# A graph, mixer and expert layer on one core: the router's mean as columns, experts chosen before their softmax, the second group turned earlier

## The reference

```python
xn = layernorm(x)
x = x + gnn(xn, src, dst) + mix(xn)              # graph attention over 206250 edges; linear mixer
x = x + ffn(layernorm(x))                        # mixture of experts, below

# ffn, with one batch of 6250 tokens, 8 experts, D = 256, F = 512:
logits = mean(x, axis=tokens) @ Wr + br          # one row of 8
routing = softmax(logits)
capacity = ceil(6250 * 1.25 / 8)                 # 977
loads = routing * 6250
scale = where(loads > capacity, capacity / loads, 1)
routing = softmax(routing * scale)
top_w, top_i = top_k(routing, 2); top_w = softmax(top_w)
h = gelu(x @ W1[e] + b1[e]); y = h @ W2[e] + b2[e]    # for the two experts
out = layernorm(sum of top_w * y + x) * gamma + beta
```

## Time and profile before

| | us |
|---|---|
| median of 3 runs | 2515.81 |
| the three runs | 2507.62, 2515.81, 2516.12 |
| profiled execution | 2508.82 |
| its span | 2507.1 |
| mean granted clock of TensorE | 0.889 |

### The profile page before, as it was taken

One profiled execution on the slowest core, in us unless ns is written; L12 is line 12 of the kernel. 1 busy time (PEld: TensorE's weight loads), 2 busy tenths in 40 slices (PEclk: granted clock), 3 DMA queues, 4 the chain that ended last, 5 costly groups with the idle time before them and its releaser, 6 DMA issues.

```text
span 2507.1 us, 32715 instructions
## 1 busy us (share of the span) xinstructions
PE 1946.2 (78%) x8711; PEld 1405.9 (56%) x8711; DVE 1652.5 (66%) x3559; ACT 962.8 (38%) x2085; POOL 1579.2 (63%) x1713
## 2 busy tenths in 40 slices
PE   8686777776776887777777678788886668899998
PEld 6454555554554555555555556666665444677776
DVE  7576766766666766676666677677777877433335
ACT  5443433333333333333333432223233546333332
POOL 5677777777777777777777777777777774000000
PEclk9889889898889788888888888898888889999999
DMA  7455555555555555555555556566555452100000
GB/s 250 137 148 149 146 146 152 146 147 148 146 144 154 145 146 151 146 144 154 145 147 151 144 161 167 158 175 167 168 166 142 135 138 75 41 19 15 16 19 27
DMA packets 164182, 330.66 MB, mean 132 GB/s; under 512 B 35700, under 2 KB 82394, under 8 KB 164014
## 3 DMA queue, kind: packets, MB, share of 16 engines
q0 software_dynamic: 78144, 220.11, 33.1%
q1 hardware_dynamic: 84418, 108.26, 14.2%
q10 hardware_dynamic: 1452, 0.38, 0.1%
HBM read 302.21 MB, written 26.39 MB: 131 GB/s over the span
## 4 chain that ended last, share of the span: by engine, by line
POOL 38%; issue 22%; PE 16%; DVE 9%; DMA 6%; POOLq 5%; DVEq 2%; ACT 1%; SPq 0%; ACTq 0%
POOL work L688 38%; PE bank L1222 7%; DMA work<-h_tab,cols 5%; POOLq L681 5%; PE bank L1212 5%; DVE work L1630 3%; PE bank L965 2%; DVE acc L1638 1%; DVE zs L1570 1%; DVEq L1551 1%; PE bank L1158 1%; DVE a2c L1572 1%; DVE a2c L1575 1%; DVE a2c L1574 0%; ACT L743 0%
## 5 line engine op out<-in xcount | busy, mean ns | idle before, releaser
L688 POOL DMA_INDIRECT work<-h_tab,cols x1612 | 1527.1, 947 | 502.0 <-issue 470.4
L1158 PE MATMUL bank<-work 128*128 128x264 f32 x3608 | 1075.6, 449 | 381.2 <-DVE work L1630 381.2
L1158 PEld LDWEIGHTS bank<-work 128*128 128x128 f32 x3608 | 773.2, 222 | 622.5 <-DVE work L1630 446.3
L1630 DVE TENSOR_TENSOR work<-work,bank 128x1024 f32<-128x1024 f32 x451 | 546.5, 1212 | 9.1 <-DVE X L1603 5.8
L791 ACT ACTIVATE bank<-a2c 128x64 f32<-128x64 f32 x226 | 51.5, 228 | 1093.7 <-DVE a2c L1577 1085.8
L1570 DVE TENSOR_REDUCE zs<-bank 128x128 f32<-128x384 f32 x226 | 125.3, 555 | 479.7 <-POOLq L677 479.4
L1464 DVE TENSOR_TENSOR work<-bank,cols 128x1024 f32<-128x1024 f32 x226 | 275.0, 1217 | 0.0
L785 ACT ACTIVATE work<-work,ones 128x1024 bf16<-128x1024 bf16 x226 | 259.5, 1148 | 7.4
L783 ACT ACTIVATE work<-work,pcol 128x1024 bf16<-128x1024 bf16 x226 | 257.4, 1139 | 10.1 <-DMA work<-dst_d 10.1
L1638 DVE TENSOR_TENSOR acc<-bank,acc 128x264 f32 x451 | 193.4, 429 | 34.9 <-PE bank L1158 32.7
L722 POOL COPY work<-acc 128x768 f32 (+2 forms) x17 | 14.0, 823 | 309.2 <-PE bank L1177 267.4
(11 more groups left out here) (300 smaller groups left out, 1929.5 us busy)
## 6 DMA issues: line engine op xcount, KB each, us to landing
work<-dst_d SPq DMA_DIRECT2D x226, 256.0 KB, 3.9
work<-h_tab,cols POOLq DMA_INDIRECT x1612
h_tab<-acc SPq DMA_DIRECT2D x49, 132.0 KB, 2.6
xnt_d<-qx_c SPq DMA_DIRECT2D x49, 128.0 KB
q2t_d<-qx_c SPq DMA_DIRECT2D x49, 128.0 KB
out<-wqkv SPq DMA_DIRECT2D x15, 384.0 KB, 2.5
X<-x SPq DMA_DIRECT2D x5, 1024.0 KB, 11.0
qx_c<-xnt_d SPq DMA_DIRECT2D x17, 128.0 KB, 3.3
```

The costliest lines, as they stand in the source:

```text
L688: nc.gpsimd.indirect_dma_start(out=work[:, (r * G + g) * TW:(r * G + g + 1) * TW], out_offset=None, in_=h_tab, in_offset=bass.IndirectOffs ...
L1158: ins = mm(bank[MB[n % len(MB)]][:, 0:TW], hot[b % HQ][:, s * G + g, :], M[n % MS][:, g, :], start=(g == 0), stop=(g == G - 1))
L1630: v.tensor_tensor(m, a, ex, ALU.mult).then_inc(msg_ready, 1)
```

## The change

The mean is summed as two columns of 128 channels: X becomes the weights, the column of rstd the moving operand, so two products per tile take the place of one, and the copy of the row and its turning go. The experts are chosen from the first softmax's weights after the cap, without the second softmax (which keeps their order); `min(w, CAPACITY / N)` takes the place of the scale. The second softmax's weights are computed later, from the chosen two, while the expert numbers are already out: the Exps become four. On ScalarE, the copies of group 0 and the b1 transfers move ahead of `normal(5, XD)`, the Gelu table behind the last Exp, the copies of group 1 ahead of hidden 0. On TensorE, the turn of group 1 moves ahead of hidden 0, and the spreading of the final weights behind it.

```diff
# ScalarE
             act.wait_ge(mean_made, 1)
-            nc.scalar.copy(sq[0:1, :], bank[7][0:1, 0:C]).then_inc(mean_kept, 1)
-            act.wait_ge(mean_made, 2)
-            nc.scalar.copy(mcol[:], bank[1][:, 16:16 + KC]).then_inc(mean_kept, 1)
+            nc.scalar.copy(mcol[:], bank[7][:, 0:KC]).then_inc(mean_kept, 1)
             normal(0, 2)
             act.wait_ge(soft_in, 1)
             nc.scalar.activation(route[:, 2, :], route[:, 1, :], ACT.Exp).then_inc(soft_out, 1)
             normal(2, 5)
             act.wait_ge(soft_in, 2)
-            nc.scalar.activation(route[:, 6, :], route[:, 5, :], ACT.Exp).then_inc(soft_out, 1)
-            normal(5, XD)
-            act.wait_ge(soft_in, 3)
-            nc.scalar.activation(route[:, 12, 0:1], route[:, 11, 0:1], ACT.Exp).then_inc(soft_out, 1)
-            nc.scalar.activation(small[0:1, 30:31], small[0:1, 31:32], ACT.Gelu)
+            nc.scalar.activation(route[:, 6, :], route[:, 7, :], ACT.Exp).then_inc(soft_out, 1)
+            x2_out(0, 0, FG)
             act.wait_ge(chosen, 1)
             for e in range(TOP):
                 n = act.value_load(route_i[0:1, e:e + 1], min_val=0, max_val=NE - 1)
                 act.dma_start(b1_sb[:, e, :], ...).then_inc(b1_loaded, 16)
+            normal(5, XD)
+            act.wait_ge(soft_in, 3)
+            nc.scalar.activation(route[:, 12, 0:1], route[:, 9, 0:1], ACT.Exp).then_inc(soft_out, 1)
+            act.wait_ge(soft_in, 4)
+            nc.scalar.activation(route[:, 12, 0:1], route[:, 11, 0:1], ACT.Exp).then_inc(soft_out, 1)
+            nc.scalar.activation(small[0:1, 30:31], small[0:1, 31:32], ACT.Gelu)
...
-            x2_out(0, 0, FG)
+            x2_out(1, 1, FG)
             act.wait_ge(b1_loaded, 16 * TOP)
             hidden(0, 0, FG, False)
-            x2_out(1, 1, FG)
             hidden(1, 1, FG, False)
# TensorE
-            row = bank[7][0:1, 0:C]
+            cols_sum = bank[7][:, 0:KC]
...
-                    mm(row, rstd[0:n, t:t + 1], X[0:n, t, :], start=(t == 0), stop=False, skip_group_check=True)
+                    for k in range(KC):
+                        mm(cols_sum[:, k:k + 1], X[0:n, t, k * P:(k + 1) * P], rstd[0:n, t:t + 1],
+                           start=(t == 0 and k == 0), stop=False, skip_group_check=True)
...
-                ins = mm(row[:, k * P:(k + 1) * P], small[:, 29:30], ones[:], start=False, stop=True, ...)
+                ins = mm(cols_sum[:, k:k + 1], ones[:], small[:, 29:30], start=False, stop=True, ...)
             ins.then_inc(mean_made, 1)
             pe.wait_ge(mean_kept, 1)
-            for k in range(KC):
-                ins = mm(bank[1][:, 16 + k:17 + k], sq[0:1, k * P:(k + 1) * P], ones[0:1, 0:1], start=True, stop=True)
-            ins.then_inc(mean_made, 1)
-            pe.wait_ge(mean_kept, 2)
...
             pe.wait_ge(soft_in, 1)
             x2_in(0, 0, FG)
-            pe.wait_ge(route_ready, 1)
-            mm(bank[4][:, 0:TOP], ones[0:1, :], route[0:1, 14, 0:TOP], start=True, stop=True).then_inc(wsel_made, 1)
+            x2_in(1, 1, FG)
...
             hidden(0, 0, FG)
-            x2_in(1, 1, FG)
+            pe.wait_ge(route_ready, 1)
+            mm(bank[4][:, 0:TOP], ones[0:1, :], route[0:1, 14, 0:TOP], start=True, stop=True).then_inc(wsel_made, 1)
# VectorE
             own(v.reciprocal(r(4, 1), r(3, 1)))
-            own(v.tensor_scalar(r(2), r(2), r(4, 1), None, ALU.mult))
-            own(v.tensor_scalar(r(4), r(2), float(N), TINY, ALU.mult, ALU.max))
-            own(v.reciprocal(r(4), r(4)))
-            own(v.tensor_scalar(r(4), r(4), CAPACITY, 1.0, ALU.mult, ALU.min))
-            own(v.tensor_tensor(r(5), r(2), r(4), ALU.mult))
-            own(v.tensor_reduce(r(3, 1), r(5), AX.X, ALU.max))
-            own(v.tensor_scalar(r(5), r(5), r(3, 1), None, ALU.subtract))
-            dve.sem_inc(soft_in, 1)
-            dve.wait_ge(soft_out, 2)
-            own(v.tensor_reduce(r(3, 1), r(6), AX.X, ALU.add))
-            own(v.reciprocal(r(4, 1), r(3, 1)))
-            own(v.tensor_scalar(r(7), r(6), r(4, 1), None, ALU.mult))
+            own(v.tensor_scalar(r(5), r(2), r(4, 1), CAPACITY / N, ALU.mult, ALU.min))
             for e in range(TOP):
...                                    # maximum, comparison, plus index, minimum: as before, on r(5) for r(7)
                 if e == 0:
+                    own(v.tensor_scalar(r(7), r(5), r(8, 1), None, ALU.subtract))
+                    dve.sem_inc(soft_in, 1)
...                                    # the first choice is taken out of the row: as before
             dve.sem_inc(chosen, 1)
-            own(v.tensor_tensor(r(11, 1), r(9, 1), r(8, 1), ALU.subtract))
+            own(v.tensor_tensor(r(9, 1), r(9, 1), r(8, 1), ALU.subtract))
             dve.sem_inc(soft_in, 1)
             dve.wait_ge(soft_out, 3)
+            own(v.tensor_reduce(r(3, 1), r(6), AX.X, ALU.add))
+            own(v.reciprocal(r(4, 1), r(3, 1)))
+            own(v.scalar_tensor_tensor(out=r(11, 1), in0=r(12, 1), scalar=-1.0, in1=r(4, 1), op0=ALU.add, op1=ALU.mult))
+            dve.sem_inc(soft_in, 1)
+            dve.wait_ge(soft_out, 4)
```

More of the change, by code:

```diff
@@ L875, in normal, with x2_out @@
                                          scale=rstd[:, t:t + 1]).then_inc(x2_ready, 1)
+            def x2_out(g, p, n):
+                act.wait_ge(x2_turned, g + 1)
+                for k in range(KC):
+                    nc.scalar.copy(x2t[p][:, k, 0:n * P], bank[k][:, 0:n * P]).then_inc(x2t_kept, 1)
             x2_root = len(LN)
@@ L903, in _ @@
                               allow_slow_non_contiguous=True).then_inc(b1_loaded, 16)
-            def x2_out(g, p, n):
-                act.wait_ge(x2_turned, g + 1)
-                for k in range(KC):
-                    nc.scalar.copy(x2t[p][:, k, 0:n * P], bank[k][:, 0:n * P]).then_inc(x2t_kept, 1)
+            normal(5, XD)
[4 more added lines that the diff above has]
+            nc.scalar.activation(small[0:1, 30:31], small[0:1, 31:32], ACT.Gelu)
             def hidden(g, p, n, roots=True):
@@ L1185, in _ @@
             for k in range(KC):
-                ins = mm(row[:, k * P:(k + 1) * P], small[:, 29:30], ones[:], start=False, stop=True, skip_group_check=True)
+                ins = mm(cols_sum[:, k:k + 1], ones[:], small[:, 29:30], start=False, stop=True, skip_group_check=True)
             ins.then_inc(mean_made, 1)
             pe.wait_ge(mean_kept, 1)
-            for k in range(KC):
-                ins = mm(bank[1][:, 16 + k:17 + k], sq[0:1, k * P:(k + 1) * P], ones[0:1, 0:1], start=True, stop=True)
-            ins.then_inc(mean_made, 1)
-            pe.wait_ge(mean_kept, 2)
             for k in range(KC):
@@ L1731, in _ @@
             own(v.reciprocal(r(4, 1), r(3, 1)))
-            own(v.tensor_scalar(r(2), r(2), r(4, 1), None, ALU.mult))
-            own(v.tensor_scalar(r(4), r(2), float(N), TINY, ALU.mult, ALU.max))
-            own(v.reciprocal(r(4), r(4)))
-            own(v.tensor_scalar(r(4), r(4), CAPACITY, 1.0, ALU.mult, ALU.min))
-            own(v.tensor_tensor(r(5), r(2), r(4), ALU.mult))
-            own(v.tensor_reduce(r(3, 1), r(5), AX.X, ALU.max))
-            own(v.tensor_scalar(r(5), r(5), r(3, 1), None, ALU.subtract))
-            dve.sem_inc(soft_in, 1)
-            dve.wait_ge(soft_out, 2)
-            own(v.tensor_reduce(r(3, 1), r(6), AX.X, ALU.add))
-            own(v.reciprocal(r(4, 1), r(3, 1)))
-            own(v.tensor_scalar(r(7), r(6), r(4, 1), None, ALU.mult))
+            own(v.tensor_scalar(r(5), r(2), r(4, 1), CAPACITY / N, ALU.mult, ALU.min))
             for e in range(TOP):
-                own(v.tensor_reduce(r(8 + e, 1), r(7), AX.X, ALU.max))
-                own(v.tensor_scalar(r(10), r(7), r(8 + e, 1), float(NE), ALU.is_lt, ALU.mult))
+                own(v.tensor_reduce(r(8 + e, 1), r(5), AX.X, ALU.max))
+                own(v.tensor_scalar(r(10), r(5), r(8 + e, 1), float(NE), ALU.is_lt, ALU.mult))
                 own(v.tensor_tensor(r(10), r(10), io, ALU.add))
@@ L1751, in _ @@
                 if e == 0:
-                    own(v.tensor_scalar(r(10), io, route[0:1, 13, e:e + 1], 4.0, ALU.is_equal, ALU.mult))
-                    own(v.tensor_tensor(r(7), r(7), r(10), ALU.subtract))
+                    own(v.tensor_scalar(r(7), r(5), r(8, 1), None, ALU.subtract))
+                    dve.sem_inc(soft_in, 1)
+                    own(v.tensor_scalar(r(10), io, route[0:1, 13, 0:1], 4.0, ALU.is_equal, ALU.mult))
+                    own(v.tensor_tensor(r(5), r(5), r(10), ALU.subtract))
             own(v.tensor_copy(route_i[0:1, 0:TOP], route[0:1, 13, 0:TOP]))
             dve.sem_inc(chosen, 1)
-            own(v.tensor_tensor(r(11, 1), r(9, 1), r(8, 1), ALU.subtract))
+            own(v.tensor_tensor(r(9, 1), r(9, 1), r(8, 1), ALU.subtract))
             dve.sem_inc(soft_in, 1)
             dve.wait_ge(soft_out, 3)
+            own(v.tensor_reduce(r(3, 1), r(6), AX.X, ALU.add))
[3 more added lines that the diff above has]
```

(1 more changed line is left out.)

## The result

| | before | after |
|---|---|---|
| median of 22 runs each | 2513.67 us | 2519.40 us |
| lowest to highest | 2507.62 to 2516.78 | 2509.45 to 2523.75 |
| profiled execution, its span | 2508.82, 2507.1 | 2517.85, 2516.1 |

The ratio of the changed kernel to the one before is 1.0021 (95% interval 1.0014 to 1.0029): slower by 5.3 us (3.5 to 7.3), clear of noise but inside the 0.5% that were called the same. The prediction said 2517 and +6.6 us.

A forecast was written before the change was run, and what follows sets the result against it. TensorE was taken as the bound from the mean's tail to the column copy, then small routing instructions on VectorE. Terms 10 - 1.05 - 2.5 + 0.15 = +6.6 on 2508.82 gave 2515.4, with 1.6 added 2517 us; range 2505 to 2531.

The forecast's parts named there:

- Mean at full clock: TensorE's 49 mean tiles: four column records take 0.47 us instead of 0.44 a tile, partly hidden in a wait; +1 us.
- Clock in the batches: Eight steps of messages and mean on TensorE: part runs at half clock, a bit more than one step; +5 us.
- (B): Rival, 13%: the alternation of messages and mean is too thin, TensorE never regains full clock; +36 us, 2545 us.
- Clock in the tail: Last 17 mean tiles, 68 records: about half at half clock, plus 0.5 us for eight records behind; +4 us.
- Column copy: Behind the mean: one ScalarE copy and one pair of products turning row into column go; -1.05 us.
- Choice: VectorE's routing: capped weights choose the experts, without an Exp and its round trip; 2.5 us earlier after the logits.
- Order: Behind the choice: first products start 1.6 us later, 1.45 us given back between the groups' products; net +0.15 us.
- The cover: W2's scaling ends near 23 us after the last conversion's start, TensorE asks for b2 near 30: 7 us spare.
- (A): Rival, 22%: weight loads count as work and the clock stays full; -2.4 us, 2506.4 us, up to 2514 for a median.
- the sign for the forecast: Granted clock from 2083 us to the mean's end: under 0.95 for the forecast, 1.0 or near 0.5 for two rivals.
- (C): Rival, 5%: the turn ahead of the first products holds them up more than it gives back; +3 us on top, 2520.
- The level: Whole kernel: profiled 2508.82 us plus 6.6 gives 2515.4; 1.6 added because a median draws from runs near 2508 and 2516.

The follow-up runs named there:

- wide form: Changed kernel with 128 equal moving columns in its column products in place of one; ratio 0.9978 against the kernel before, median 2501.58 us.
- the experiment that isolates it: Changed kernel with 128 equal moving columns for the 32 tiles inside the batches, one for the tail's 17; ratio 0.9999 against the kernel before.

## Why the prediction was right

- **Mean at full clock, +1 (0 to 1.5).** The pace of a record was read nearly right (0.118 us from L1190, 0.114 measured), and 17 tiles take 7.75 us against 7.50 (128-column form). But inside the batches the column form is quicker: at full clock a step of messages and mean takes 3.57 us (2112.34 to 2115.90 and on), in the kernel before 3.79. Over eight steps that is -1.8, with the tail -1.5: the term lies below its lower bound. The forecast priced the mean's records alone; the time from a message product to the mean behind it shrank too (1.87 against 1.97 us).
- **Clock in the batches, +5 (0 to 31).** The batches grew by 7.1 us in the profiled pair. The clock alone cost more, about 10 us: from the first mean record to the tail 39.98 us, where the wide form at full clock took 32.10 with 2.4 us of waits in it. The quicker steps, and waits that the kernel before had there (1.3 us), give the rest back. So +1 was too high and +5 too low, and that 6 is near 7.1 is partly luck. The mechanism was right: with the array fed throughout by 128 columns the clock stays, by one it goes, at the same loads. What I took from the mix of the gather stretch was an average; the profiles show runs of several steps at one level (24 us at half here), which also fits the spread of the times, 14.3 us for the changed kernel and 9.2 for before; that the spread comes from it was not tested. Once at half the alternation tends to stay there, as rival (B) had it, but it comes back after about 24 us, here and with the columns alone. The argument against (B), that one dense run of 3.9 us at half would bring the clock back, failed: three of 3.87 us, each between column groups, did not. Why it comes back when it does is open.
- **Clock in the tail, +4 (0 to 7.6).** 11.99 us against 7.7 and 0.99 against 0.50: +4.8 here, +4.3 in the experiment that isolates it.
- **Column copy, -1.05.** The copy into mcol now starts 0.04 us behind the closing products, where the copy of the row started; the detour of 1.05 us is gone whole. The tail's and this term together: +3.9 in the table.
- **Choice, -2.5.** 6.68 to 4.32 us, -2.4; the meeting with GpSimd's copy was where it was expected (0.56 instead of 0.22 us).
- **Order, +0.15 (-1.5 to +2).** +1.0 ahead of the first products (forecast +1.6: ScalarE was free 2.8 us after the conversion's start and not 3.05, and turn and drain took 1.3 us and not 1.55) and -2.6 behind them: -1.5 in the pair, at the end of the bound, -0.8 by the means over the ten kernels. The cover held: W2 was scaled by 2165.7, b2's product came at 2171.8.
- **Rivals.** (A), the clock stays full, is ruled out by the clock itself, 0.69 from 2083 to the last mean record (the sign for the forecast was under 0.95), and by the two pairs that differ in columns alone. With it goes the rule of no idle gaps (the Trainium skill, TensorE: Matmul & The Clock Gate, section Why this matters for your kernels) as the only condition: TensorE's records fill 24.00 of 24.00 us at a clock of 0.52. (B) was right in the manner, not the length. (C) did not come.
- **The level.** 2517 rested on a base of 2510.4 (the profiled execution and 1.6 us for where a median falls) and +6.6. Over 22 runs the base was 2513.67, and the difference by the ratio +5.3; the two errors partly cancel, which is luck as well.

## What to carry to other kernels

In this kernel a product with one moving column cost its weight load, 0.11 us a record at full clock and 0.21 soon after, and it took the dense products around it down as well: count moving columns, not TensorE's busy share, when a reduction is moved onto weights. If such a form saves a step elsewhere, try to widen its moving side with repeated columns until they take as long as the next load; with 128 of them it was free here and held the clock, with 32 it did not always. A microsecond won ahead of the first dense products of a new phase may only move them ahead of the clock's rise.

## What the runs showed of the hardware that was not expected

- Useless columns made TensorE faster: 68 records 11.52 us with one moving column, 7.75 us with 128, behind the same batches.
- A wait of 0.30 us (the column mean alone) or of 0.62 and 0.75 us (32 columns) behind a thin group of the mean was followed by the lower level, though a wait of 0.28 us in the 32-column form was not; with 128 columns waits of 1.84 and 0.54 us, and of 2.33 us in the form with a thin tail, left it full.
- The column form with a full clock is quicker than the row form inside the batches, 3.57 against 3.79 us a step, though it has twice the records.
- GpSimd's copy of 128x768 stretched VectorE's neighbours on one partition from 0.22 to 0.56 us (TENSOR_SCALAR) and from 0.15 to 0.67 us (TENSOR_TENSOR), up to the copy's end each time.
